# Two graph layers that take in the row sums, norms, gate logits and projections: one kernel of a two-layer graph and expert network, before and after

## The reference

```
def gnn(x, adj, W, b):                     # twice, the second with a relu
    d = adj.sum(axis=1) ** -0.5            # row sums of adj
    return (d[:, None] * adj * d[None, :]) @ x @ W + b

x = x + gnn0(layernorm(x))                 # layer 0
x = x + moe(layernorm(x), gate, top 2 of 8)
x = x + relu-gnn1(layernorm(x))            # layer 1
x = layernorm(x); kept = x
h = layernorm(x) * g + b
q, k, v = h @ wq + bq, h @ wk + bk, h @ wv + bv
x = x + bo + softmax(q k' / sqrt(32)) v @ wo       # 8 heads, over all tokens
x = x + kept + moe(layernorm(x), router, top 2 of 8 with a capacity)
```

## Time and profile before

| | us |
|---|---|
| median of 3 runs | 3116.29 (3116.19 to 3118.62) |
| the profiled execution | 3114.11 |
| its span in the profile | 3112.5 |

### The profile page before, as it was taken

The page is one execution under the profiler, slowest core; times in us unless marked ns, Lnnn a source line. Parts: engine busy times, 40 slices in busy tenths (PEclk is TensorE's granted clock), DMA queues, the critical chain, the costliest instruction groups (busy, mean ns, idle before and its releaser), DMA issues. The chain is left out here.

```text
span 3112.5 us, 54672 instructions
## 1 busy us (share of the span) xinstructions
PE 2461.9 (79%) x20856; PEld 1917.1 (62%) x20856; DVE 2020.7 (65%) x2826; ACT 1512.1 (49%) x2617; POOL 1194.6 (38%) x674
## 2 busy tenths in 40 slices
PE   0299950899993399945799999999999999327993
PEld 0288840899993388844366666666666665227993
DVE  7944540788884744463777777777777773436884
ACT  0233320677762333343266666666666666215771
POOL 0100006000004300011288888888888888330003
PEclk9999955899996699978699999999999999558996
DMA  9865402666662555337100000030000000115663
GB/s 410 356 251 175 126 1 88 237 232 229 244 225 93 218 176 171 108 120 198 41 15 15 15 10 13 15 81 15 10 13 15 15 12 3 44 41 215 238 235 113
DMA packets 140110, 375.94 MB, mean 121 GB/s; under 512 B 22033, under 2 KB 82705, under 8 KB 121873
## 3 DMA queue, kind: packets, MB, share of 16 engines
q1 hardware_dynamic: 122928, 319.82, 29.2%
q0 software_dynamic: 15696, 48.77, 4.4%
q10 hardware_dynamic: 1296, 4.75, 0.4%
HBM read 314.30 MB, written 58.98 MB: 120 GB/s over the span
## 5 line engine op out<-in xcount | busy, mean ns | idle before, releaser
L1256 DVE TENSOR_REDUCE at_part_max<-ps_x 128x2 f32<-128x1024 f32 x624 | 734.1, 1220 | 265.0 <-PE ps_x L1159 265.0
L1106 POOL TENSOR_TENSOR at_pool_sum<-at_pool_sum,at_probs 128x1024 f32<-128x1024 f32 x364 | 865.8, 2379 | 95.3 <-ACT at_probs L1227 54.1
L1227 ACT ACTIVATE at_probs<-ps_s 128x512 f32<-128x512 f32 x1352 | 698.3, 604 | 340.5 <-PE ps_s L1121 306.6
L1121 PE MATMUL ps_s<-at_qst,at_kst 97*128 97x256 f32 x2704 | 518.1, 311 | 5.3 <-ACT at_probs L1227 4.6
L1121 PEld LDWEIGHTS ps_s<-at_qst,at_kst 97*128 97x128 f32 x2704 | 369.3, 190 | 218.2 <-ACT at_probs L1227 113.4
L461 PE MATMUL ps_acc<-adj_hi,y_hi 128*128 128x512 f32 (+1 forms) x728 | 280.2, 385 | 229.9 <-DVE adj_lo L508 229.9
L1138 PE MATMUL ps_oz<-at_probs,k_xhat 128*32 128x256 f32 (+1 forms) x5408 | 392.0, 386 | 0.0
L508 DVE TENSOR_TENSOR adj_lo<-adj_raw,adj_hi 128x1024 fp32r<-128x1024 f32 (+1 forms) x182 | 207.5, 1147 | 240.3 <-ACT adj_hi L430 240.3
L430 ACT ACTIVATE adj_hi<-adj_raw 128x1024 fp32r<-128x1024 f32 (+1 forms) x182 | 181.9, 999 | 309.9 <-PE ps_acc L463 279.9
L461 PEld LDWEIGHTS ps_acc<-adj_hi,y_hi 128*128 128x128 f32 x728 | 138.5, 190 | 257.9 <-issue 230.0
L831 POOL DMA_DIRECT2D results<-ex_res x54 | 38.7, 717 | 646.8 <-DVE ex_res L818 646.8
(11 more groups left out here) (181 smaller groups left out, 4046.7 us busy)
## 6 DMA issues: line engine op xcount, KB each, us to landing
ex_w<-w SPq DMA_DIRECT2D x108, 1024.0 KB, 6.8
adj_raw<-adjT SPq DMA_DIRECT2D x156, 512.0 KB, 4.2
adj_rows<-adj SPq DMA_DIRECT2D x26, 1664.0 KB, 10.7
slots<-zeros POOLq DMA_DIRECT2D x27, 512.0 KB, 21.5
ex_rows<-slots SPq DMA_DIRECT2D x54, 256.0 KB, 2.9
results<-ex_res POOLq DMA_DIRECT2D x54, 256.0 KB, 2.7
at_qst<-qk_parts SPq DMA_DIRECT2D x78, 128.0 KB, 2.5
ex_b<-b SPq DMA_DIRECT2D x54, 128.0 KB, 2.1
```

The lines of the kernel that those rows point to most:

```text
L1106: pool.tensor_tensor(pool_sum[:, g % 2], pool_sum[:, g % 2], probs[:, tile % RING], ALU.add).then_inc(pool_added, 1)
L1121: last = pe.matmul(ps_s[:, unit % S_BANKS, hh, :], kst[:, 2 * j + hh, k * P:(k + 1) * P], qst[:, g % 2, 2 * j + hh, :], start=True, stop=True)
L1227: act.activation(probs[:, tile % RING, 2 * j:2 * j + 2], ps_s[:, unit % S_BANKS], ACT.Exp, scale=scale).then_inc(taken, 1)
L1256: dve.tensor_reduce(part_max[:, g % 2, heads, qt, kc], ps_x[:, pair, :], AX.X, ALU.max).then_inc(x_free, 1)
```

## The change

The row sums, the norms, the gate logits and the projections lose their blocks and become part of the two graph layers; the start of attention is reordered.

- **Layer 0.** `constants` and `inverse_roots` are gone. The jobs of the first four chunks are interleaved, piece by piece: `(0, pc), (1, pc), (2, pc), (3, pc)`, then chunks 4, 5 and 6 one after the other. All eight banks hold the four accumulators. The row tiles `2pc+2` and `2pc+3` of `adj` are loaded on SP's queue between the pieces, into the two halves of `xhat`, which is free here, and are summed on ACT by a copy with an accumulated output (L407), one group ahead of the pieces that need them. Their roots, `y` and its split are made two row tiles at a time. The raw ring is 5.
- **Behind each chunk,** at fixed positions in the order of pieces (`at_positions`), each engine does a step of: times W, take, row statistics, root, norm applied (ACT), and in layer 0 turn, copy, gate logits for two row tiles at once. In layer 1 the chain is longer: `x` normalised in place, kept in memory (POOL's queue), statistics again, second norm, turn, copy, the projections of each row tile (one bank pair, so the product of tile k+1 waits for `split` of tile k), the store on POOL's queue. The raw ring is 4. After the last piece the positions go on, for up to 30 more.
- **Slots.** Both sets of expert slots are zeroed in layer 0, after the first four chunks.
- **Attention.** The first keys are loaded in seven pieces, each with its own semaphore; the queries of block 1 go behind the stacked keys; PE waits for `wo` only before its first use. `MAX_AHEAD` 17 to 15, `ROW_AT` 10 to 11, `OUT_AT` 11 to 12.

```diff
+def piece_order(first):
+    together = 4 if first else 0
+    jobs = [(c, pc) for pc in range(PIECES) for c in range(together)]
+    jobs += [(c, pc) for c in range(together, CHUNKS) for pc in range(PIECES)]
+    ends = [jobs.index((c, PIECES - 1)) for c in range(CHUNKS)]
+    if first:
+        turns = [ends[together - 1] + 6 * c for c in range(CHUNKS - 1)] + ends[-1:]
...
+    evacuations = at_positions([(ends[c] + 4, c) for c in range(CHUNKS)])
+    w_products = at_positions([(at + 1 + 2 * q, (c, q, p)) for at, c, p, q in pairs])
+    takes = at_positions([(at + 6 + 2 * q, (c, p)) for at, c, p, q in pairs])
...
+        turned_at = at_positions([(at + 12 + 3 * q, p) for at, c, p, q in pairs])
+        copied_at = at_positions([(at + 17 + 4 * q, p) for at, c, p, q in pairs])
+        produced_at = at_positions([(at + 14 + 4 * q + 2 * i, 2 * p + i) for at, c, p, q in pairs for i in range(2)])
+        taken_at = at_positions([(at + 19 + 4 * q + 2 * i, 2 * p + i) for at, c, p, q in pairs for i in range(2)])
...
         def _(sp):
+            def load_rows(i):
+                if i >= 2:
+                    sp.wait_ge(summed, i - 1)
+                sp.dma_start(adj_rows[:, i % 2, :], t["adj"][i * P:(i + 1) * P, :]).then_inc(rows_loaded[i % 2], 16)
...
+                if first and c in (0, 2) and 2 * pc + 2 + c // 2 < NT:
+                    load_rows(2 * pc + 2 + c // 2)
+                if g >= raw_ring:
+                    sp.wait_ge(lo_made, g - raw_ring + 1)
...
+            def sum_rows(pc):
+                for i in (2 * pc, 2 * pc + 1):
+                    act.wait_ge(rows_loaded[i % 2], i // 2 * 16 + 16)
+                    act.activation(adj_rows[:, i % 2, :], adj_rows[:, i % 2, :], ACT.Copy, accum_out=m.deg[:, i:i + 1]).then_inc(summed, 1)
...
+                    if first and c == 0 and pc + 1 < PIECES:
+                        sum_rows(pc + 1)
+                    if not first and c == 0:
+                        round_rows(pc)
+                    round_piece(g)
+                    if first and c == 1 and pc + 1 < PIECES:
+                        root_degrees(pc + 1)
+                    if first and c == 3 and pc + 1 < PIECES:
+                        round_rows(pc + 1)
...
+            def produce(k):
+                pe.wait_ge(copied, k // 2 + 1)
...
+                if k:
+                    pe.wait_ge(split, k)
...
+            def take_product(k):
+                dve.wait_ge(produced, k + 1)
+                dve.tensor_tensor(m.xhat[:, k, :], ps_v[:, 0:D], m.rows[:, 4, :], ALU.add)
+                dve.wait_ge(read, k + 1)
+                if k >= 2:
+                    dve.wait_ge(qk_kept[k % 2], k // 2 * 32)
+                for g in range(G):
+                    last = dve.scalar_tensor_tensor(qk_lo[:, k % 2, g, :], ps_qk[:, g * P:(g + 1) * P], m.cols[:, 4 + g:5 + g],
+                                                    qk_hi[:, k % 2, g, :].bitcast(F32), ALU.add, ALU.subtract)
+                last.then_inc(split, 1)
...
-MAX_AHEAD, ROW_AT, DIVIDE_AT, DIVIDE_PARTS, MULTIPLY_AT, OUT_AT = 17, 10, 1, 8, 18, 11
+MAX_AHEAD, ROW_AT, DIVIDE_AT, DIVIDE_PARTS, MULTIPLY_AT, OUT_AT = 15, 11, 1, 8, 18, 12
...
             load_queries(0)
-            load_keys(0)
-            load_queries(1)
+            for kc in range(KC):
+                cols = slice(kc * KEYS, min(NP, (kc + 1) * KEYS))
+                sp.dma_start(keys[:, 0, cols].bitcast(F32), m.qk[0, HG, :, cols]).then_inc(first_keys[kc], 16)
+            sp.wait_ge(first_keys[KC - 1], 16)
             load_query_stack(0)
...
             pe.wait_ge(ones_row, 1)
-            pe.wait_ge(wo_loaded, 16)
```

More of the change, by code:

```diff
@@ L271, in _ @@
             act.wait_ge(applied, 1)
-            if keep is not None:
-                act.wait_ge(kept, 16)
             for k in range(DVE_SHARE, NT):
@@ new lines, with first_tile, chunk_tiles @@
+PAST_END = 30
+def first_tile(c):
+    return min(NT, c * RCHUNK // P)
+def chunk_tiles(c):
+    return range(first_tile(c), first_tile(c + 1))
+def piece_order(first):
[5 more added lines that the diff above has]
+        turns = [ends[together - 1] + 6 * c for c in range(CHUNKS - 1)] + ends[-1:]
+        banks = [c if c < together else c - together & 1 for c in range(CHUNKS)]
+    else:
+        turns, banks = ends, [c & 1 for c in range(CHUNKS)]
+    return jobs, ends, turns, banks
@@ new lines, in store @@
+            def store(k):
+                pool.wait_ge(split, k + 1)
+                for n, part in enumerate((qk_hi, qk_lo)):
+                    pool.dma_start(m.qk[n, :, :, k * P:(k + 1) * P].rearrange("g p n -> p g n"), part[:, k % 2].bitcast(F32))\
+                        .then_inc(qk_kept[k % 2], 16)
+            keep(0)
+            for c in range(CHUNKS):
+                add_output_bias(c)
+                if c + 1 < CHUNKS:
+                    keep(c + 1)
+                for k in chunk_tiles(c):
+                    store(k)
@@ new lines, in root, with apply @@
+            def root(c, which):
+                at = slice(first_tile(c), first_tile(c + 1))
+                n = which + (c if first else 2 * c)
+                act.wait_ge(moments, n + 1)
+                act.activation(m.rs[:, at], m.var[:, at], ACT.Sqrt).then_inc(rooted, 1)
+            def apply(p, src, dst, done, n):
+                act.wait_ge(scaled, n)
+                for k in (2 * p, 2 * p + 1):
+                    act.activation(dst[:, k, :], src[:, k, :], ACT.Identity, bias=m.shift[:, k:k + 1], scale=m.rs[:, k:k + 1]).then_inc(done, 1)
@@ L467, in _, with times_w @@
-            rows_times_w(len(widths) - 1)
+            def times_w(c, q, p):
+                pe.wait_ge(evacuated, max(c + 1, together))
+                if p:
+                    pe.wait_ge(taken, 2 * p)
+                for i in range(2):
+                    at = slice((2 * q + i) * P, (2 * q + i + 1) * P)
+                    for j in range(KT):
+                        last = pe.matmul(ps_w[:, i * D:(i + 1) * D], sums[:, c % SUMS, j, at], w[:, j, :], start=j == 0, stop=j == KT - 1)
+                last.then_inc(multiplied, 1)
@@ L513, in _ @@
+            counts.settle(dve)
             dve.wait_ge(chain, NT)
```

695 lines of the change are left out of this document (386 added, 309 removed).

## The result

| | us |
|---|---|
| before, median of 4 runs | 3116.55 (3116.19 to 3118.62) |
| after, median of 4 runs | 3032.98 (3027.1 to 3038.4) |
| ratio, 95% interval | 0.973 (0.971 to 0.9751) |
| forecast | 3009 (2966 to 3046) |
| the profiled execution of after | 3030.24, span 3028.3 |

A forecast was written before the change was run, and what follows sets the result against it. Transfers bound 20 to 120 us, PE both layers and attention proper. Layer 0 -91, layer 1 +12 and attention's start -28.6 make -107: 3114.1 profiled becomes 3007, the median 2.2 above it, 3009 us (2966 to 3046).

The forecast's parts named there:

- Layer 0, the start: Start to routes: PE starts near 37 us, first product ends about 207, routes begin at 356.5 instead of 447.5, -91.
- The group of four: Layer 0's first product: four pieces and two row tiles, 5.50 MB, take 12.95 us, set by the transfers.
- ACT has 12.95 - 11.2 = 1.8 us to spare: Layer 0's first product: ACT's work is 11.2 us of a 12.95 us group, so the transfers set it.
- the group of four is longer: Rival, layer 0: two-row ring and SP's queue lose 2.6 us each group, 34 in all: 3043 us; chance 0.17.
- The rate: Layer 0's first product: transfers from memory move at 425 GB/s.
- Layer 1, up to the last piece: Layer 1 from PE's start at 1059.6 us: product, W, projections, turns and a 40 us wait end at 1418.
- The wait on `split`: Layer 1 projections: the next tile's product waits for the one before, sharing one bank pair; 40 us, bounds 0 and 60.
- The tail: Layer 1 after the last piece: six tiles in series and the last pair's norms, 44 us, up to 50 at 1.2 GHz.
- rival 4: PE's clock falls in both layers, 100 us in layer 0 and 94 in layer 1: 3203 us; chance 0.04.
- Attention: Start of attention: PE starts 11.5 us into the block and 30 jobs follow, not 34, together -28.6; body +0.2.
- No wait in layer 1: Rival: the forecast 40 us wait in layer 1 does not come, or is small: 2969 us; chance 0.14.
- ACT sets the group at 17 us: Rival, layer 0: a sum takes twice a copy, 5.9 us, so a group takes 17.1: 3059 us; chance 0.07.

The follow-up runs named there:

- ring7: `all_together` with seven raw buffers for layer 0's pieces instead of five; 2963.44 us, ratio 0.9518.
- lag4: The changed kernel, with ACT and DVE taking a projected row tile four pieces behind its product instead of five; 3018.03 us, ratio 0.9692.
- tail_banks: `lag4` with a second pair of accumulators for odd row tiles after layer 1's last piece; 2999.14 us, ratio 0.9637.
- keep_later: `tail_banks` with POOL storing the next chunk's x behind the first two projected tiles' stores; 2984.99 us, ratio 0.9582.
- all_together: `keep_later` plus y rounded between sums, ones row waited for later, block 1 queries before the stacks, projection weights behind layer 1's fourth piece; 2967.74 us, ratio 0.9526.

## Why the prediction was right, and where its sizes were off

- **Layer 0, the start.** PE started at 39.6 us (forecast 37), the first product's sums were emptied at 210.7 (207), the last 13 us were as forecast (12.5). 6.6 us are missing of 91. That it is so few is in part luck: the last row's sum began at 188.4 us where I had its row landed at 178, 10 late, but from there to the emptied sums it took 22.3 us and not 29, since fewer than eight pieces were left for PE. With groups of 13.2 us `ring7` has the routes at 350.9, 5.6 before my 356.5.
- **The group of four.** "ACT has 12.95 - 11.2 = 1.8 us to spare" is the step that was wrong. ACT's work was well sized (10.7 us; a sum 2.97 us, forecast 2.96), but I counted work and not waits: 0.42 and 1.86 us for DVE in a fixed order make its period 12.95 us. Then nothing is to spare, each late row delays the pieces, each late piece buffer stops SP, and the queue runs low. The rival "the group of four is longer" had the part of this mechanism that is SP's queue and the rings, and not ACT's waits; the size was 1.05 us a group, not 2.6. Shown by taking away either side (12.95 and 13.2 us), and by `y` between the sums with the ring of seven (13.2).
- **The rate.** The mean was 391 GB/s in after and 419 to 420 once the queue stayed full, which is the forecast's 425 within 1.5%. The Trainium skill, "DMA: Bandwidth & Descriptors", section "Where 436 GB/s comes from", gives about 358 GB/s for a core's transfers between memory and SBUF, as its half of what two cores share; by that a group would be 15.4 us. The same section names 425 GB/s as measured for 16 MB. This kernel runs on one core, and where the queue was kept full, at 381 to 420 GB/s, it was nearer to the second number.
- **Layer 1, up to the last piece.** The wait on `split` came, by the mechanism forecast: 29.5 us against 40. The sum of the work, 318.5 us, is also right: without the wait the stretch lasted 323.5. What was left out is that PE works longer for the same matmuls where it has waits: from the first to the last piece 326.9 us with the 15 waits of after, 329.5 and 327.0 with the 5 of `lag4` and `tail_banks`, 319.4 without, in `keep_later`. So this doesn't grow with the number of waits. And PE's start was 2.8 us late, since ACT waited for the first piece behind three weight loads. Together the last piece came 6 us later than forecast.
- **The tail** is the term that was mis-sized: 55.7 us where I took 44 (up to 50 at the lower level). I had the serial walk, but took a tile at 2.55 + 1.14 + 1.13 = 4.8 us, at the full clock. The six products of after:

```profile
1340.86 2.00 PE L558 MATMUL ps_acc<-xt,wqk 128*128 128x128 f32 x16
1346.21 2.02 PE L558 MATMUL ps_acc<-xt,wqk 128*128 128x128 f32 x16 [2.05 <-DVE qk_lo L665]
1351.58 3.46 PE L558 MATMUL ps_acc<-xt,wqk 128*128 128x128 f32 x16 [2.49 <-DVE qk_lo L665]
1358.40 3.47 PE L558 MATMUL ps_acc<-xt,wqk 128*128 128x128 f32 x16 [2.49 <-DVE qk_lo L665]
1371.04 3.78 PE L558 MATMUL ps_acc<-xt,wqk 128*128 128x128 f32 x16 [1.11 <-ACT xt L453]
1378.37 3.64 PE L558 MATMUL ps_acc<-xt,wqk 128*128 128x128 f32 x16 [2.49 <-DVE qk_lo L665]
```

  The first two take the 2.0 us of the earlier trace rows, and a tile's period is 5.4 us; the other four take 3.46 to 3.78, and the period is 6.8 and 7.3. So of the 11.7 us that are too many, some 7 are slow matmuls (the same 136 are busy for 28.9 us here and for 21.8 with two pairs of accumulators), some 3, by my estimate, are six tiles of 5.4 instead of 4.8 us at the full clock, and the rest is not resolved. The Trainium skill, "TensorE: Matmul & The Clock Gate", section "HAM oscillation — how this bites in real kernels", has a loop that waits for a transfer before each group of matmuls and runs every group at the slow clock. The trace agrees in part: the waits here are for DVE and ACT, and the product behind the first of them was still fast. It cost 7 us in the tail, where I had 6 for it, and 7.5 in the layer before, where rival 4 had 94.
- **Attention.** The start was right to 0.4 us, and for the reasons given: PE waited for the row of ones, 30 jobs followed at 1.13 us. The body, forecast at +0.2, came out 1.5 to 4.1 us longer in the kernels above.
- **No wait in layer 1, ACT sets the group at 17 us, the clock falls**: none came.

## What to carry to other kernels

When two engines or queues with nearly the same period are tied by a short ring, count the waits in each one's order, not its work: 12.95 us and 13.2 us made 14.0 here, and one wait filled and two more buffers gave it back. A step merged into another's loop is worth only what its position in every queue allows; here the same merged layer cost 29 us or gained 19, by two positions and one pair of banks. A short wait of TensorE has to be priced with the slow matmuls that can follow it, though no fixed price for one wait came out here.

## What the runs showed of the hardware

- A copy of 128 x 3328 with accumulated output took 2.97 us on ACT and a separate read of the accumulator 0.18 us, mostly hidden: sums follow each other at 2.97 us.
- Two kinds of transfers on one queue, 13 KB and 4 KB packets, moved 420 GB/s; with all in 3.3 and 4 KB packets, and more issues, 381 GB/s (391 in after, which differs from it in this alone).
- Two holes of some 2 us in the queue of transfers hardly show in the DMA share over 120 us (0.98 at 395 GB/s in `all_together`, 1.01 at 419 in `ring7`); they show in the rate of slices under 1 us (18 and 52 GB/s).
- In layer 1 the same 1631 matmuls were busy for 326.9 to 329.5 us in three kernels in which PE had 5 or 15 waits for DVE's `qk_lo` of up to 4.5 us between them, and for 319.4 us in the one without.
